# Second attention of a two-layer cross-attention: another order of five steps within a round

## The reference

```
# x, ctx: 32 batches x 256 tokens x 256 features, float32
x = x + attention_16_heads(x @ Wq.T, ctx @ Wk.T, ctx @ Wv.T)[0]   # batch 0 only, added to all
X = layernorm(ctx, norm1);  F = layernorm(x, norm2)
attended = softmax(F @ X.T * scale) @ X                           # first attention of the second layer
h = gelu(attended @ fc1.T + fc1_b)                                # 4 hidden values a token
cross = h @ fc2.T + fc2_b                                         # 256 features of rank 4 plus bias
n = layernorm(cross, norm3)
self = softmax(n @ n.T * scale) @ n                               # second attention
out = F + gamma2 * (cross + gamma1 * self)
```

## Time and profile before

| | |
|---|---|
| median of 3 runs | 345.43 us (344.05 to 349.63) |
| profiled execution, its own time | 346.67 us |
| span of the trace | 344.8 us |
| second attention in the trace | 248.2 us to 312.1 us |
| busy in the span: TensorE, VectorE, ScalarE, GpSimd | 270.3, 222.6, 154.2, 122.5 us |

### The profile page before, as it was taken

One profiled execution on the slowest core, in us unless ns is written; L12 is line 12 of the kernel. 1 busy time (PEld: TensorE's weight loads), 2 busy tenths in 40 slices (PEclk: granted clock), 3 DMA queues, 4 the chain that ended last, 5 costly groups with the idle time before them and its releaser, 6 DMA issues.

```text
span 344.8 us, 6187 instructions
## 1 busy us (share of the span) xinstructions
PE 270.3 (78%) x1838; PEld 202.8 (59%) x1838; DVE 222.6 (65%) x678; ACT 154.2 (45%) x329; POOL 122.5 (36%) x189
## 2 busy tenths in 40 slices
PE   5799821789999999999999999950177888882990
PEld 4666511678999899999999989940022222220330
DVE  6446555789778767777877773249754334526992
ACT  1256500437565557765555777540053443330330
POOL 8000025637766657776666774002500000000000
PEclk9969985596999899999999999975555555555555
DMA  6400000453345553443555420100000000000798
GB/s 220 178 0 2 1 3 10 143 183 121 124 130 180 183 183 112 162 140 139 178 183 182 139 105 31 63 1 0 0 2 0 0 2 0 2 1 0 297 362 317
DMA packets 19313, 35.11 MB, mean 102 GB/s; under 512 B 2272, under 2 KB 2272, under 8 KB 19296
## 3 DMA queue, kind: packets, MB, share of 16 engines
q1 hardware_dynamic: 19296, 34.89, 29.4%
HBM read 18.11 MB, written 8.39 MB: 77 GB/s over the span
## 4 chain that ended last, share of the span: by engine, by line
PE 32%; DVE 24%; issue 19%; POOL 12%; DMA 5%; ACT 4%; SPq 1%; POOLq 0%; DVEq 0%; ACTq 0%
PE psum L782 8%; DVE Fall L509 5%; PE psum L772 5%; DMA xN<-x 5%; DVE nm L462 5%; POOL zc L560 4%; PE psum L876 4%; POOL zy L560 4%; POOL xN L553 4%; PE psum L810 4%; PE psum L789 3%; PE psum L846 2%; PE psum L798 2%; DVE bn L380 2%; PE psum L884 1%
## 5 line engine op out<-in xcount | busy, mean ns | idle before, releaser
L553 POOL TENSOR_TENSOR xN<-xN,tgt 128x512 f32<-128x512 f32 x32 | 40.5, 1267 | 93.2 <-DVE rstd L355 46.9
L782 PE MATMUL psum<-XT,FT 128*128 128x256 f32 x256 | 65.0, 400 | 0.0
L782 PEld LDWEIGHTS psum<-XT,FT 128*128 128x128 f32 x256 | 49.4, 203 | 6.1
L630 ACT ACTIVATE E<-psum,nmax 128x256 f32<-128x256 f32 x64 | 27.3, 487 | 57.3 <-DVE nmax L411 57.3
L618 ACT ACTIVATE FT<-psum,par 128x256 f32<-128x256 f32 x64 | 32.8, 568 | 24.0 <-PE psum L772 23.6
L789 PEld LDWEIGHTS psum<-fc1s,XT 128*128 128x128 f32 x256 | 34.1, 194 | 4.4 <-DVE V L416 2.7
L380 DVE BATCH_NORM_STATS2 bn<-cN 128x6 f32<-128x256 f32 x64 | 24.1, 418 | 19.5 <-POOL xN L553 19.3
L560 POOL TENSOR_SCALAR zc<-cN,nmean,rstd 128x256 f32<-128x256 f32 x64 | 34.8, 553 | 3.0 <-PE psum L772 3.0
L772 PE MATMUL psum<-ident,zc 128*128 128x128 f32 x128 | 21.8, 296 | 17.0 <-POOL zy L560 12.3
L560 POOL TENSOR_SCALAR zy<-xN,nmean,rstd 128x256 f32<-128x256 f32 x64 | 35.1, 557 | 0.0
L623 ACT ACTIVATE XT<-psum,b1s,w1s 128x256 f32<-128x256 f32 x64 | 32.9, 577 | 0.0
(11 more groups left out here) (153 smaller groups left out, 419.1 us busy)
## 6 DMA issues: line engine op xcount, KB each, us to landing
cN<-ctx SPq DMA_DIRECT2D x32, 256.0 KB, 2.6
xN<-x SPq DMA_DIRECT2D x32, 256.0 KB, 2.9
Fall<-FT SPq DMA_DIRECT2D x32, 256.0 KB, 3.0
out<-Fall SPq DMA_DIRECT2D x32, 256.0 KB, 3.1
x0T<-x0t SPq DMA_DIRECT2D x1, 256.0 KB, 3.0
wqT<-wqt SPq DMA_DIRECT2D x1, 256.0 KB, 3.3
c0T<-c0t SPq DMA_DIRECT2D x1, 256.0 KB, 3.5
wkT<-wkt SPq DMA_DIRECT2D x1, 256.0 KB, 4.8
```

What stands on the lines that cost most here:

```text
L553: pool.tensor_tensor(xN[:, slot, :], xN[:, slot, :], tgt2[:, :, :].rearrange("p t d -> p (t d)"), ALU.add).then_inc(y_ok, 1)
L630: act.activation(E[:, j % 2, t * N:(t + 1) * N], bank[2 + j % 2][:, t * N:(t + 1) * N], ACT.Exp, bias=nmax[:, j % 2, t:t + 1]).then_inc(ex ...
L782: last = pe.matmul(bank[2 + j % 2][:, t * N:(t + 1) * N], FT[:, j % 2, c, t * P:(t + 1) * P], XT[:, j % 2, c, :], start=c == 0, stop=c == ...
```

## The change

Each of the three loops gets another order within a round. On TensorE `scores(p + 2)` becomes the first step of round p, ahead of `maxima_turn(p + 1)` and of `attend` or `back`. On VectorE `maxima(p)` comes ahead of `collected` and `returned`. On ScalarE `weights(p)` comes ahead of `maxima_turned(p + 1)`. No instruction is added or taken away, and no semaphore wait is changed in what it asks.

```diff
@@ vector @@
         for p in range(PAIRS + 3):
+            if p < PAIRS:
+                maxima(p)
             if p % 2 == 0 and p >= 4:
                 collected((p - 4) // 2)
             if p % 2 == 1 and p >= 5:
                 returned((p - 5) // 2)
-            if p < PAIRS:
-                maxima(p)
             if p % 2 == 0 and 2 <= p < PAIRS - 1:
                 turned(p + 1)
@@ scalar @@
         for p in range(PAIRS):
+            weights(p)
             if p + 1 < PAIRS:
                 maxima_turned(p + 1)
-            weights(p)
             if p % 2 == 1 and p + 3 < PAIRS:
                 turned(p + 3)
@@ tensor @@
         for p in range(PAIRS + 2):
+            if p + 2 < PAIRS:
+                scores(p + 2)
             if p + 1 < PAIRS:
                 maxima_turn(p + 1)
             if p % 2 == 0 and p >= 2:
                 attend(p // 2 - 1)
             if p % 2 == 1 and p >= 3:
                 back((p - 3) // 2)
-            if p + 2 < PAIRS:
-                scores(p + 2)
             if p + 1 < PAIRS:
                 shift(p + 1)
```

## The result

The first measurement gave 349.11 us as the median of 4 runs (348.45 to 349.42), against 346.0 us for 4 runs of the kernel before (344.05 to 349.63): ratio 1.0106, 95% interval 1.0057 to 1.0156. So the kernel was measured 1% slower, and the time lies 0.5 us above the range of the prediction. In 12 more runs of the same changed kernel, timed beside 29 of the kernel before, the medians were 347.0 and 348.08 us: ratio 0.9974, interval 0.9927 to 1.0021. The slowdown didn't come back, and the profiles show where most of it lay.

A forecast was written before the change was run, and what follows sets the result against it. TensorE was taken as nearest to the bound, its idle time as waits for operand copies. Start +1.24, steady rounds -0.40 and end -0.84 gave 0.0 us, so a median of 345.4 us, range 343.0 to 348.6.

The forecast's parts named there:

- the range: Whole kernel: median expected within 343.0 to 348.6 us, given 90%.
- The waits end with the operand copy, not with the maxima: Second attention: TensorE's idle 1.35 us a period ends with the operand copy; after the change 0.69 and 0.59 before scores.
- The steady rounds gain 0.07 us a period: Second attention, rounds 2 to 13: idle time 1.28 us where 1.35 stood, TensorE's work unchanged; 0.4 us over 5.5 periods.
- The start costs 1.24 us: Second attention's start: table load and first exponential delay the second copy of maxima and shift(1); head of round 2 late.
- the sum: Start, steady rounds and end together: +1.24 - 0.40 - 0.84 = 0.0 us.
- The table load: ScalarE at the start: 1.28 us right behind the first copy, exponential directly after, no added drain of about 1.38 us.
- The end gives 0.84 back: Last rounds: round 13 opens 0.84 us late, but maxima_turn(15) and all behind it keep their times.
- a wait for the maxima in round 14: Last rounds on TensorE: pair 15's maxima stay the one real wait for maxima, so maxima_turn(15) starts at 304.96 as before.
- The clock rival: Second attention: denser order gets TensorE's full clock instead of 0.50; six periods give -16, 329 us; chance 2%.
- The starting value, 345.43: Median in us of the kernel before, to which the predicted change of 0.0 us was applied.

The follow-up runs named there:

- the order that covers the copies: Changed kernel with TensorE's round reordered: scores, shift of the pair before, turn, attend or back, then transpose of the newest maxima; 339.74 us, ratio 0.976 to the kernel before.

## Why the prediction was right, and where it was wrong

- **The waits end with the operand copy, not with the maxima**: shown. The idle time moved to the scores with 0.69 and 0.52 us (0.69 and 0.59 forecast), and the order that covers the copies took most of it away.
- **The steady rounds gain 0.07 us a period**: 0.09 measured. The idle time fell by 0.14 us, and TensorE's own work, taken as unchanged, grew by 0.05, so the closeness is in part luck.
- **The start costs 1.24 us**: the head of round 2 stands at 12.75 us after the stage's start; before it stood at 11.60 (259.84 minus 248.24). That is 1.15, on the path of the sum: load, exponential, second copy, `shift(1)`. Behind it stands a second path of the same height, the banks that the first exponential frees for the scores of pair 3. The sum didn't need it, but it is why undoing ScalarE's part alone gave nothing back.
- **The table load** starts 0.01 us behind the copy before it (which ends at 255.71) and ends 0.02 us ahead of its exponential: 255.72 to 257.00, then 257.02. That is by the row; the drain that the Trainium skill adds to each load (ScalarE: Activation LUTs, "What ACT_TABLE_LOAD costs") has no room in this trace either.
- **The end gives 0.84 back**: round 13 opened 0.64 us late (54.59 against 53.95), and `maxima_turn(15)` came at 56.53 us, 0.19 earlier than before, where I had 0.0. I had kept a wait for the maxima in round 14; none is left there. The scores of pair 15 start at 304.81, their maxima end at 306.68 (305.46 + 1.22), and TensorE's own steps fill the time until 306.75. The sum of the change was right to 0.2 us.
- **The clock rival**: the granted clock stayed at 0.50 in this stage, even with TensorE busy 7.69 of 8 us.
- **What failed is the step from the sum to the median**, in the range. I wrote that a median of a few runs moves by part of the spread, as if runs lay around one value. They lie in groups 2.3 us apart. Between the upper two the traces show the difference, how long the clock stays low in the heads. A median of four can fall wholly into the top one, and it did: 349.11 against an upper end of 348.6. The three runs shown of before lay one in or near each group (344.05, 345.43, 349.63), and I took this for noise around the middle. The range should have gone at least to the highest of them, 349.63. The starting value, 345.43, was of the same kind: two later sets of 29 runs of the kernel before had medians of 348.08 and 346.34.

Not settled: why all four of the first runs fell in that group. In the two later sets of 29 runs of the kernel before 15 and 11 did, so four in a row have a chance of 2 to 7% (0.38 or 0.52 to the fourth) if runs are independent; no run here tests that. Open too are what sets the first group apart, why the same eight products of the start took 2.24 us in one trace and 2.98 in another, and what sets the later low stretches.

## What to carry to other kernels

Before moving a step ahead of a wait, look at what all the conditions of that wait are: an idle row names one releaser, and a second one as late as the first inherits the gap. A dependent step gains by work that stands between producer and consumer, so put the other steps between them; moving the consumer to the front only renames the wait. Where runs of one kernel fall into groups, compare stage lengths in the traces, or group with group, since the median of a few runs measures the mix, and an interval made from them doesn't know of it. The mean granted clock helps to sort them but isn't enough: runs at 0.781 and at 0.782 lay 2 us apart here.

## What the runs showed of the hardware

- One and the same kernel had TensorE's clock low (1.2 GHz) for 6.8 us in one execution and for 13.6 us in another. The fall came in or right behind an idle time of 1.7 us of TensorE at about 16 us, in all eight traces without the four products. The heads took 31.8 us in the one and 34.9 in the other. Four products whose result nobody reads, in that idle time, kept the clock at 2.4 GHz through the heads in all three traces, which took 29.4 us each.
- ScalarE's table load of 1.28 us followed the copy before it within 0.02 us, and its exponential followed it within 0.02 us.
- The second attention ran at 0.50 in every trace, even with TensorE busy 96% of the time; its lengths repeat to 0.03 us from trace to trace (56.53 and 56.53, 56.72 and 56.75).
